# A two-layer attention and feed-forward kernel: the pieces of four engines put into another order from the second group's softmax on

## What is computed

```python
x = x + xattn16(norm(x), ctx)          # 16 heads of 16, softmax over 77 keys
h = norm(x)
x = x + layernorm(h + relu(h @ w1 + b1) @ w2 + b2) * gamma + beta     # 256 -> 1024 -> 256
x = x + xattn1(layernorm(norm(x)), layernorm(ctx))                    # one head, 77 keys
x = x + y_all[idx]   # of 8 matrices the one that the row's position selects
```

## Time and profile before

| what | us |
|---|---|
| median of 3 runs (lowest, highest) | 271.42 (271.34, 272.66) |
| time of the profiled execution | 271.57 |
| its span, first to last instruction | 269.7 |
| TensorE busy | 247.4 (92%) |
| VectorE busy | 218.2 (81%) |
| GpSimd busy | 189.6 (70%) |
| ScalarE busy | 160.7 (60%) |

### The profile page before, as it was taken

The page is one execution under the profiler, slowest core; times in us unless marked ns, Lnnn a source line. Parts: engine busy times, 40 slices in busy tenths (PEclk is TensorE's granted clock), DMA queues, the critical chain, the costliest instruction groups (busy, mean ns, idle before and its releaser), DMA issues.

```text
span 269.7 us, 6211 instructions
## 1 busy us (share of the span) xinstructions
PE 247.4 (92%) x2048; PEld 219.3 (81%) x2048; DVE 218.2 (81%) x573; ACT 160.7 (60%) x510; POOL 189.6 (70%) x361
## 2 busy tenths in 40 slices
...
GB/s 167 319 319 121 0 79 2 2 39 12 70 0 43 39 166 187 5 21 2 0 2 39 101 39 57 63 80 40 2 218 55 2 0 2 0 1 4 0 156 156
DMA packets 11156, 17.61 MB, mean 65 GB/s; under 512 B 1377, under 2 KB 7509, under 8 KB 11125
## 3 DMA queue, kind: packets, MB, share of 16 engines
...
...
## 4 chain that ended last, share of the span: by engine, by line
PE 70%; DVE 13%; POOL 5%; issue 4%; ACT 4%; DMA 2%; SPq 0%; POOLq 0%; DVEq 0%
PE PB L275 33%; PE PB L268 13%; PE PB L472 7%; PE PB L348 5%; PE S L396 5%; PE PB L408 4%; PE S L386 4%; ACT E L1067 2%; DVE SX L666 2%; DMA WKV<-in_w_k 2%; POOL E L1261 1%; DVE SX L680 1%; POOL SM L1218 1%; DVE XTL L645 1%; POOL out_x L1314 1%
## 5 line engine op out<-in xcount | busy, mean ns | idle before, releaser
L1261 POOL TENSOR_TENSOR E<-E,SX 128x308 f32<-128x308 f32 x64 | 43.9, 712 | 10.0 <-DVE SX L683 9.8
L1067 ACT ACTIVATE E<-S,SX 128x77 f32<-128x77 f32 x128 | 39.4, 337 | 10.7 <-DVE SX L666 10.7
L275 PE MATMUL PB<-XTH,W1H 128*128 128x256 f32 x128 | 37.3, 291 | 1.6 <-DVE XTL L645 1.4
L275 PE MATMUL PB<-W2H,HH 128*128 128x256 f32 x128 | 37.5, 293 | 0.0
L275 PE MATMUL PB<-W2H,HL 128*128 128x256 f32 x128 | 35.7, 279 | 0.0
L275 PE MATMUL PB<-W2L,HH 128*128 128x256 f32 x128 | 35.7, 279 | 0.0
L275 PE MATMUL PB<-XTL,W1H 128*128 128x256 f32 x128 | 35.6, 278 | 0.0
L275 PE MATMUL PB<-XTH,W1L 128*128 128x256 f32 x128 | 35.5, 278 | 0.0
L1218 POOL TENSOR_TENSOR SM<-SM,nhalf 128x2 f32<-128x2 f32 x40 | 28.4, 711 | 3.1
L1090 ACT ACTIVATE HH<-PB 128x512 fp32r<-128x512 f32 x32 | 19.1, 600 | 15.9 <-PE PB L275 15.6
L1077 ACT ACTIVATE EW<-S 124x640 f32<-124x640 f32 x32 | 21.9, 711 | 10.8 <-PE S L396 10.7
...
## 6 DMA issues: line engine op xcount, KB each, us to landing
...
```

What stands on the lines that cost most here:

```text
L275: t = e.matmul(dst, a, b, start=first and j == 0, stop=last and j == n - 1)
L1067: t = e.activation(Ei[:, h * NK:(h + 1) * NK], P[:, at:at + NK], ACT.Exp, bias=SX[:, i, 0, k:k + 1], accum_out=SX[:, i, 1, k:k + 1])
L1261: t = e.tensor_tensor(Eh, Eh, SX[:, i, 2, 8 * a + h:8 * a + h + 4].unsqueeze(2).to_broadcast([128, 4, NK]), ALU.mult)
```

## The change

Only the four lists are laid anew, from the second group's softmax on; the functions are untouched, so each engine issues the same instructions as before, in another order, and some TensorE pieces write to another of the four buffers. No piece before `tE(0,0,0)` on TensorE moves; SyncE's list is the same. The core of the diff, with the moves that the text speaks of:

```diff
@@ tensor
-            sc(0, 1, 0, 1); sc(0, 1, 1, 0); q(1, 1); tA(2, 3); tE(0, 0, 0, 0); tE(0, 0, 1, 1); tE(0, 1, 0, 0)
-            sc(1, 0, 0, 1); sc(1, 0, 1, 0); vrep(1, 1); q(2, 2); tE(0, 1, 1, 0); sc(1, 1, 0, 1); pv(0, 0, 0); pv(0, 1)
-            sc(1, 1, 1, 0); wo(0, 3); f_turn(0); r_rank(2); tE(1, 0, 0, 0); tE(1, 0, 1, 1); tE(1, 1, 0, 0)
-            sc(2, 0, 0, 1); sc(2, 0, 1, 0); f_kv(0, 0); pv(1, 0, 2); f_kv(1, 3); tE(1, 1, 1, 0); tB(0, 0)
-            sc(2, 1, 0, 1); sc(2, 1, 1, 0); pv(1, 1); r_perm(1); w1(0, 0, 3); wo(1, 0); w1(0, 1, 2); w1(0, 2, 1)
-            w1(0, 3, 3); f_m(0); tE(2, 0, 0, 0); tA(3, 2); w2(0, 0, 0, 1); tE(2, 0, 1, 1); tB(1, 0); w2(0, 0, 1)
-            w2(0, 1, 0); q(3, 2); w2(0, 1, 1); w1(1, 0, 3); sc(3, 0, 0, 1); sc(3, 0, 1, 0); w1(1, 1, 0); w1(1, 2, 2)
+            sc(0, 1, 0, 1); sc(0, 1, 1, 0); q(1, 1); tA(2, 3); tE(0, 0, 0, 0); vrep(1, 0); tE(0, 0, 1, 1)
+            tE(0, 1, 0, 0); sc(1, 0, 0, 1); sc(1, 0, 1, 0); q(2, 3); pv(0, 0, 1); tE(0, 1, 1, 0); sc(1, 1, 0, 1)
+            f_turn(0); pv(0, 1); sc(1, 1, 1, 0); wo(0, 1); r_rank(3); tE(1, 0, 0, 1); f_kv(0, 2); tE(1, 0, 1, 1)
+            tE(1, 1, 0, 0); sc(2, 0, 0, 1); sc(2, 0, 1, 0); f_kv(1, 0); pv(1, 0, 3); tB(0, 1); tE(1, 1, 1, 1)
+            sc(2, 1, 0, 0); tA(3, 2); pv(1, 1); sc(2, 1, 1, 1); r_perm(1); wo(1, 3); w1(0, 0, 0); w1(0, 1, 1)
+            w1(0, 2, 3); w1(0, 3, 2); f_m(0); tB(1, 1); tE(2, 0, 0, 1); f_q(0); w2(0, 0, 0, 3); q(3, 1); tE(2, 0, 1, 0)
+            w2(0, 0, 1); w2(0, 1, 0); w2(0, 1, 1); w1(1, 0, 2); sc(3, 0, 0, 0); sc(3, 0, 1, 1); w1(1, 1, 1); w1(1, 2, 2)
...
-            w1(7, 3, 1); w2(7, 0, 0, 0); tD(3, 1); w2(7, 0, 1); w2(7, 1, 0); w2(7, 1, 1); tD(4, 3); tC(6, 1); pr(1, 2)
-            cs(6, 0); pr(2, 3); pr(3, 1); tC(7, 0); cp(6, 2); cs(7, 0); co(6); pr(4, 0); cp(7, 3); tD(5, 2); co(7)
+            w2(7, 0, 1); w2(7, 1, 0); w2(7, 1, 1); tC(6, 2); tD(3, 0); pr(1, 1); tD(4, 2); cs(6, 0); pr(2, 3); pr(3, 2)
+            cp(6, 0); tC(7, 1); co(6); cs(7, 1); pr(4, 2); cp(7, 3); tD(5, 0); co(7); pr(5, 1); tD(6, 3); pr(6, 2)
@@ vector
-            ssum(0, 1, 0); r_ranks(); ql(1); r_expert(); ssum(0, 1, 1); smax(1, 0, 0); lo("A", 2); smax(1, 0, 1)
-            f_kv(0); f_kv(1); vb(1); lo("B", 0); ssum(2, 0, 0); smax(2, 1, 0); smax(2, 1, 1); kbl(1); r_index()
-            ssum(2, 0, 1); apply("A", 3); hl(0, 0); hl(0, 1); x1(1); ssum(2, 1, 0); stats("B", 1); hl(0, 2); f_m()
-            hl(0, 3); apply("B", 1); lo("A", 3); r_pairs(); lo("B", 1); ssum(2, 1, 1); ql(3); y(0); stats("A", 4)
+            ssum(0, 1, 0); r_ranks(); ssum(0, 1, 1); ql(1); lo("A", 2); stats("A", 3); smax(1, 0, 0); f_norm()
+            ssum(2, 0, 0); apply("A", 3); f_kv(0); f_kv(1); lo("B", 0); kbl(1); smax(2, 1, 0); r_index(); x1(1)
+            lo("A", 3); stats("B", 1); hl(0, 0); ssum(2, 0, 1); apply("B", 1); hl(0, 1); smax(2, 1, 1); f_m(); hl(0, 2)
+            hl(0, 3); lo("B", 1); r_pairs(); ql(3); stats("A", 4); smax(3, 0, 0); ssum(2, 1, 0); hl(1, 0); y(0)
@@ scalar
-            apply("A", 3); o(1); ex(2, 0, 1); ex(2, 1, 0); hh(0, 0); hh(0, 1); ex(2, 1, 1); hh(0, 2); hh(0, 3); kba(1)
+            ex(2, 0, 1); et(1, 1, 1); hi("A", 3); o(1); w_hi(4); hh(0, 0); hh(0, 1); ex(2, 1, 0); apply("B", 1)
@@ gpsimd
-            rs("B", 0); en(1, 1, 1); w_lo(3); w_lo(4); en(2, 0, 0); bo(2); en(2, 0, 1); en(2, 1, 0); rs("B", 1); gx(4)
-            gx(6); be(0); b2(0); b2(1); en(2, 1, 1); rs("A", 4); rs("Y", 0); gx(5); en(3, 0, 0); en(3, 0, 1); rs("C", 0)
+            rs("B", 0); en(1, 1, 1); en(2, 0, 0); b2(0); w_lo(3); bo(3); rs("B", 1); w_lo(4); b2(1); en(2, 0, 1); gx(4)
+            gx(6); be(0); gx(5); en(2, 1, 0); en(2, 1, 1); rs("A", 4); gx(7); rs("Y", 0); be(1); en(3, 0, 0); rs("A", 5)
...
-            rs("D", 3); be(6); b2(7); rs("Y", 6); rs("D", 4); bd(2); bd(3); rs("C", 6); rs("D", 5); be(7); rs("Y", 7)
-            bd(4); rs("C", 7); rs("D", 6); bd(5); rs("D", 7); bd(6); bd(7); put(0); put(1); put(2); put(3); put(4)
+            rs("D", 3); be(6); rs("D", 4); rs("Y", 6); be(7); bd(2); b2(7); rs("C", 6); rs("D", 5); bd(3); rs("Y", 7)
+            rs("C", 7); bd(4); rs("D", 6); rs("D", 7); bd(5); bd(6); bd(7); put(0); put(1); put(2); put(3); put(4)
```

More of the change, by code:

```diff
@@ L964, in vector @@
             smax(0, 0, 1); f_stats(); lo("A", 1); ssum(0, 0, 0); smax(0, 1, 0); smax(0, 1, 1); ssum(0, 0, 1); vb(0)
-            ssum(0, 1, 0); r_ranks(); ql(1); r_expert(); ssum(0, 1, 1); smax(1, 0, 0); lo("A", 2); smax(1, 0, 1)
-            stats("A", 3); ssum(1, 0, 0); ssum(1, 0, 1); f_norm(); smax(1, 1, 0); ql(2); smax(1, 1, 1); x1(0)
+            ssum(0, 1, 0); r_ranks(); ssum(0, 1, 1); ql(1); lo("A", 2); stats("A", 3); smax(1, 0, 0); f_norm()
+            smax(1, 0, 1); vb(1); ssum(1, 0, 0); r_expert(); smax(1, 1, 0); ql(2); ssum(1, 0, 1); smax(1, 1, 1); x1(0)
@@ L972, in vector @@
[L972 to L991, removed]
@@ new lines, in vector @@
+            ssum(2, 1, 1); smax(3, 0, 1); f_q(); stats("Y", 0); hl(1, 1); f_c(); hl(1, 2); smax(3, 1, 0); apply("A", 4)
+            hl(1, 3); ssum(3, 0, 0); stats("A", 5); smax(3, 1, 1); ssum(3, 0, 1); lo("A", 4); x2(0); x1(2)
+            stats("B", 2); ssum(3, 1, 0); stats("A", 6); apply("A", 5); ssum(3, 1, 1); f_o(); apply("B", 2); y(1)
+            stats("Y", 1); stats("C", 0); ql(4); x2(1); lo("B", 2); smax(4, 0, 0); smax(4, 0, 1); lo("A", 5)
+            apply("C", 0); x1(3); hl(2, 0); stats("A", 7); stats("B", 3); ssum(4, 0, 0); ssum(4, 0, 1); ql(5)
@@ new lines, in vector @@
+            smax(4, 1, 0); hl(2, 1); apply("A", 6); hl(2, 2); stats("C", 1); apply("B", 3); hl(2, 3); smax(4, 1, 1)
+            apply("C", 1); cm(0); ssum(4, 1, 0); lo("B", 3); ssum(4, 1, 1); smax(5, 0, 0); starts(); y(2); hl(3, 0)
+            stats("Y", 2); smax(5, 0, 1); hl(3, 1); hl(3, 2); ssum(5, 0, 0); smax(5, 1, 0); ssum(5, 0, 1); x2(2)
+            lo("A", 6); x1(4); ssum(5, 1, 0); stats("C", 2); hl(3, 3); smax(5, 1, 1); stats("B", 4); apply("A", 7)
+            apply("C", 2); cm(1); x3_(0); y(3); ssum(5, 1, 1); apply("B", 4); ql(6); stats("Y", 3); cm(2); x2(3)
@@ new lines, in vector @@
+            lo("A", 7); smax(6, 0, 0); stats("C", 3); smax(6, 0, 1); x3_(1); lo("B", 4); smax(6, 1, 0); x3_(2); x1(5)
+            apply("C", 3); ssum(6, 0, 0); hl(4, 0); ssum(6, 0, 1); stats("B", 5); smax(6, 1, 1); hl(4, 1); hl(4, 2)
+            cm(3); apply("B", 5); ql(7); hl(4, 3); ssum(6, 1, 0); ssum(6, 1, 1); lo("B", 5); x3_(3); smax(7, 0, 0)
+            smax(7, 0, 1); y(4); stats("Y", 4); hl(5, 0); x2(4); stats("D", 0); hl(5, 1); hl(5, 2); stats("C", 4)
+            apply("D", 0); ssum(7, 0, 0); hl(5, 3); ssum(7, 0, 1); smax(7, 1, 0); stats("D", 1); smax(7, 1, 1)
@@ new lines, in vector @@
+            ssum(7, 1, 0); apply("C", 4); ssum(7, 1, 1); apply("D", 1); x1(6); stats("B", 6); y(5); stats("Y", 5)
+            apply("B", 6); x2(5); cm(4); lo("B", 6); x1(7); stats("C", 5); pa(0); stats("D", 2); stats("B", 7); hl(6, 0)
+            apply("B", 7); hl(6, 1); apply("C", 5); hl(6, 2); hl(6, 3); stats("D", 3); lo("B", 7); apply("D", 2); x3_(4)
+            y(6); stats("Y", 6); apply("D", 3); cm(5); stats("D", 4); hl(7, 0); hl(7, 1); x2(6); hl(7, 2); hl(7, 3)
+            x3_(5); stats("C", 6); stats("D", 5); apply("C", 6); y(7); stats("Y", 7); apply("D", 4); x2(7)
@@ L995, in scalar @@
+            stats("C", 7); cm(6); pa(1); apply("C", 7); apply("D", 5); pa(2); pa(3); cm(7); x3_(6); stats("D", 6); pa(4)
+            x3_(7); apply("D", 6); stats("D", 7); pa(5); pa(6); apply("D", 7); pa(7); pa(8); pa(9); pa(10); pa(11)
+            pa(12); pa(13); pa(14)
         def scalar(e):
@@ new lines, in scalar @@
+            hh(0, 2); hh(0, 3); hi("B", 1); et(2, 0, 0); ex(2, 1, 1); qh(3); kba(1); et(2, 0, 1); hh(1, 0); ex(3, 0, 0)
+            hh(1, 1); hh(1, 2); et(2, 1, 0); et(2, 1, 1); hh(1, 3); apply("A", 4); ex(3, 0, 1); ex(3, 1, 0); hi("A", 4)
+            o(2); ex(3, 1, 1); starts(); apply("A", 5); et(3, 0, 0); apply("B", 2); et(3, 0, 1); qh(4); et(3, 1, 0)
+            et(3, 1, 1); hi("A", 5); hi("B", 2); o(3); ex(4, 0, 0); hh(2, 0); ex(4, 0, 1); hh(2, 1); qh(5)
+            apply("C", 0); hh(2, 2); xtc(0); apply("A", 6); apply("B", 3); hh(2, 3); ex(4, 1, 0); apply("C", 1)
```

93 lines of the change are left out of this document (42 added, 51 removed).

## The result

The changed kernel takes 274.43 us (median of 12 runs, 272.44 to 276.12), the kernel before 271.70 beside it (12 runs). The ratio is 1.0091, with a 95% interval of 1.0061 to 1.0121: slower by 0.9%, outside the predicted 265.8 to 270.4. The profiled execution took 276.12 us (span 274.3), the slowest of the twelve; 0.9 us of what it has over the profile of before lies behind the last product, in the stores.

What follows compares the result with a forecast made beforehand. TensorE, 92% busy, could only win back waiting, with VectorE setting the pace in the first stretch. 2.5 + 0.3 - 0.5 + 1.5 = 3.8 us won gave 267.6 us against the median, range 265.8 to 270.4.

Steps and rivals of the forecast that it cites:

- first stretch: From 29.2 to 75.1 us, behind the front: TensorE was to reach w1(1,0) earlier, a lead of 2.5 us.
- middle: From 100 to 230 us, TensorE full: 0.3 won by fewer changes of product kind, 0.5 charged for late feeders.
- tail: From w2(7)'s end on: a shorter x2(7) and less waiting in the last group's chain, 1.4 to 1.5 us won.
- `ql(3)` should end at 75.1 - 1.1 - 1.0 = 73.0: VectorE, first stretch: 1.1 from two ssum moved behind ql(3), 1.0 from waits for hi(B,0) and wo(0) gone.
- each feeder ready: Middle: walking both lists to the eighth group found TensorE's inputs ready in time, at several places with margins under 0.3.
- the gain at `x2(7)`: Tail: with bd(4) behind rs(C,7) on GpSimd, x2(7)'s second half takes 0.88 instead of 1.76, 0.9 shorter.
- the lead of 2.1: VectorE, first stretch: the 1.1 and 1.0 us by which ql(3) was to end earlier than 75.1.
- The wait of 1.4 us goes: TensorE, first stretch: its wait for lo(B,1) ahead of w1(1,0) vanishes, since lo(B,1) moves ahead of r_pairs.
- `w_lo(4)` ending near 63: GpSimd, first stretch: w_lo(4) behind rs(B,1) ends at 63.1, about when w2(0,0,0) wants it, at no cost.
- the signs named as wrong: TensorE waits for en or hl from 75 to 200 us, w_lo(4) after 66, or tC(7) over 8 us behind w2(7).
- The charge of 0.5: Middle: 0.5 us lost to feeders with thin margins; bounds 0 and 2.5, the whole lead from the first stretch.
- rival 3: GpSimd's list, first stretch: w_lo(4) behind rs(B,1) comes late and TensorE stalls; slower, 273.5 us, chance 0.08.

Runs made afterwards that it cites:

- with the runs broken up: Changed kernel with GpSimd's bo(2), bo(3), bo(7), be(4) later and VectorE's x2(2) ahead of hl(3,2): 270.26 us, ratio 0.9958 to the kernel before.
- GpSimd's list alone mended: Changed kernel with only GpSimd's list altered (bo(2), bo(3), bo(7), be(4) later), VectorE's list kept: 271.85 us, ratio 1.0024 to the kernel before.
- the last run: Kernel with the runs broken up, plus r_expert ahead of ssum(1,0,0) and w_lo(2) behind en(1,0,0): 272.01 us, ratio 0.9997 to the kernel before.

## Why the prediction was wrong

Its terms, each as us won against the kernel before, by the same reckoning (`f_q` and `tD(3)` counted where they are done):

```
                       predicted   changed kernel   with the runs broken up
first stretch             2.5          -0.4                 1.0
middle                   -0.2          -3.9                -0.5
tail                      1.5           0.7                 0.7
```

The last column is the kernel with `x2(2)` moved as well. Each is one profile: by the same reckoning, counted from `sc(0,1,0)`, the first stretch gives 1.0 there and 1.6 with GpSimd's list alone mended, although their lists are the same in it; the 0.58 and 1.28 of `r_expert` account for the difference.

- **The step that failed** is the one that both stretches rest on: "So `ql(3)` should end at 75.1 - 1.1 - 1.0 = 73.0", and "each feeder ready" in the middle. Each moved piece was given the duration that it had at its old place. In these pieces the duration goes with what GpSimd does beside them: `r_expert`'s small instruction took 2.62 us and not 0.22, `x2(2)` 4.49 and not 1.79. Over all instructions of VectorE that take over 1.4 times what their line and form take undisturbed the excess is some 6 us in the profile of before, 13 in the changed kernel and 9 with the runs broken up (to about 1 us, by what is taken for undisturbed); a good part of it is one-input `TENSOR_SCALAR`. I had the sentence ("where `bo`, `be`, `bd` now meet another `x2`, a loss of the same size") and let it price one place, the gain at `x2(7)`; I did not walk GpSimd's list beside VectorE's for the others.
- **First stretch, VectorE.** The order came as walked; `r_expert` took 2.4 us more and `f_norm` 0.6, and the lead of 2.1 became a lag of 0.2. Whether the walk would have held without them is answered by the last run: no. GpSimd's `en` and `w_lo` bound the front as well, and the 2.5 were too large by more than half.
- **First stretch, TensorE.** "The wait of 1.4 us goes" was right and worth nothing by itself; the sentence behind it, that `ql(3)` is late next, was the whole matter.
- **`w_lo(4)`.** "`w_lo(4)` ending near 63" was off: 66.21, one of the signs named as wrong. It cost no wait of its own, since `f_m` was late by about as much.
- **Middle.** The charge of 0.5 had its upper bound at 2.5, "the whole lead". A wait can cost more than a lead: the 2.0 us at `cs(1)` cost 3.7 by the estimate above, as the clock fell behind it. With the runs broken up the middle costs 0.5, near the charge; 0.8 of it is one wait, for `en(5,1,1)`.
- **Tail.** `bd(4)` behind `rs(C,7)` was right in kind and size (0.88). The other 0.6 were not there: `tC(7)` came at 7.97, not 7.7, and `pr(4)` waited 0.22 for `pa(3)`, which VectorE does behind `apply(D,5)` and `pa(2)`.
- **Rivals.** The time came out on the side of rival 3 but not by its mechanism; the collision of `bo` with `x2` was no rival and should have been one, on the slower side.

The Trainium skill's page "SBUF — State Buffer", section "Who interferes with whom", says that whichever of the two issues first has the shared pair for its whole instruction. The pairs of 0.9 us in `x2(7)` before and in `x2(3)` agree. The 2.62 us of `r_expert` and the 2.70 in `x2(2)` do not: there VectorE waited through up to three further instructions of GpSimd. Why an instruction waits for one of GpSimd's at one time and for the whole run at another stays open. The place does not decide it alone: behind the same pieces, begun at the same distance, one wait ended after one instruction (0.58) and the other after two (1.28). So what the runs show is that the hold-up comes with GpSimd's instructions on SBUF and is gone without them (0.22 in the last experiment); how long it is they don't explain.
